# Eighteen weight pieces of a fused attention and FFN kernel: lower ternary side on GpSimd, joined on VectorE

## The reference

```
x = x + cross_attention(layernorm(x), ctx)      # two inner layernorms, one head of width 512, softmax over 256
x = x + ffn(layernorm(x))

def _bitlinear(x, w_latent):                    # used twice in the ffn
    scale = clip(mean(abs(w_latent), axis=1, keepdims=True), 1e-05, None)
    tern = clip(round(w_latent / scale), -1.0, 1.0)
    return x @ (tern * scale).T
h = _bitlinear(x, w_fc) + gate * (x @ v.T @ fast_b.T @ u.T)
y = _bitlinear(relu(h)**2, w_proj)              # w_fc (2048, 512), w_proj (512, 2048)
```

## Time and profile before

| | us |
|---|---|
| median of 3 runs (lowest, highest) | 805.66 (803.67 to 807.49) |
| the profiled execution, its own time | 805.04 |
| its span, from the first to the last instruction | 803.0 |

### The profile page before, as it was taken

How to read it: one execution, slowest core, us unless ns; L and a number is a source line. 1 busy time by engine, 2 the same in 40 slices (tenths; PEclk the granted TensorE clock), 3 DMA queues, 4 the chain that set the end, 5 groups by cost and what they waited for, 6 DMA issues and landing times.

```text
span 803.0 us, 10829 instructions
## 1 busy us (share of the span) xinstructions
PE 777.0 (97%) x3877; PEld 642.9 (80%) x3877; DVE 543.3 (68%) x1100; ACT 374.9 (47%) x705; POOL 150.0 (19%) x171
## 2 busy tenths in 40 slices
PE   6999988999999999999999999999999999999998
PEld 4678767887888778887888788887888788888886
DVE  5998857667757685577766685577766686476434
ACT  5997545335551644326542554326542554424332
POOL 3241130112202022022201122012301122012001
PEclk9999999999999999999999999999999999999999
DMA  9753141034410551134410452124420441021001
GB/s 314 273 144 102 17 77 56 36 54 69 127 40 1 85 112 53 40 46 69 118 57 1 70 86 94 40 36 74 98 83 0 70 75 55 0 35 45 27 0 53
DMA packets 180554, 56.93 MB, mean 71 GB/s; under 512 B 167666, under 2 KB 168068, under 8 KB 180500
## 3 DMA queue, kind: packets, MB, share of 16 engines
q1 hardware_dynamic: 150368, 51.51, 26.2%
q10 hardware_dynamic: 30132, 4.73, 3.4%
HBM read 27.64 MB, written 8.39 MB: 45 GB/s over the span
## 4 chain that ended last, share of the span: by engine, by line
PE 77%; SPq 6%; DVE 5%; ACT 3%; ACTq 3%; DMA 3%; issue 2%; DVEq 0%
PE G L1183 23%; PE O L1299 22%; PE H L1318 22%; SPq L505 5%; ACTq L788 3%; PE H L1324 3%; DVE rbuf L1074 2%; DMA Wv_s<-in_L_xattn_Wv_dram 2%; ACT rbuf L749 1%; PE H L1167 1%; PE G L1265 1%; PE O L1372 1%; DMA n_blocks<-n_rows 1%; PE H L1183 1%; ACT qbuf L757 1%
## 5 line engine op out<-in xcount | busy, mean ns | idle before, releaser
L1299 PE MATMUL O<-projT,qbuf 128*128 128x512 f32 x992 | 246.9, 391 | 6.7 <-DVE qbuf L1078 6.7
L1299 PEld LDWEIGHTS O<-projT,qbuf 128*128 128x128 f32 x992 | 184.1, 188 | 47.7 <-DVE qbuf L1078 10.6
L757 ACT ACTIVATE qbuf<-rbuf 128x512 fp32r<-128x512 f32 x125 | 79.1, 633 | 148.5 <-DVE rbuf L1074 112.1
L1074 DVE TENSOR_TENSOR rbuf<-rbuf 128x512 f32<-128x512 f32 x128 | 95.5, 746 | 61.9 <-ACT rbuf L749 61.8
L1318 PE MATMUL H<-even_group,fcT 128*128 128x512 f32 x512 | 127.8, 392 | 2.9 <-ACT rbuf L749 2.9
L1318 PE MATMUL H<-odd_group,fcT 128*128 128x512 f32 x512 | 127.3, 391 | 0.0
L749 ACT ACTIVATE rbuf<-H,scf 128x512 f32<-128x512 f32 x128 | 86.9, 679 | 68.2 <-PE H L1324 63.2
L1318 PEld LDWEIGHTS H<-even_group,fcT 128*128 128x128 f32 x512 | 94.9, 188 | 22.4 <-ACT rbuf L749 3.3
L1078 DVE TENSOR_TENSOR qbuf<-rbuf,qbuf 128x512 fp32r<-128x512 f32 x125 | 88.8, 710 | 33.7 <-ACT qbuf L757 30.9
L1318 PEld LDWEIGHTS H<-odd_group,fcT 128*128 128x128 f32 x512 | 95.3, 188 | 19.3
L1183 PE MATMUL G<-Wvo,tT 128*128 128x512 f32 x270 | 65.6, 391 | 0.0
(11 more groups left out here) (196 smaller groups left out, 1066.9 us busy)
## 6 DMA issues: line engine op xcount, KB each, us to landing
xb<-in_x_dram SPq DMA_DIRECT2D x8, 1024.0 KB, 4.8
n_blocks<-n_rows SPq DMA_DIRECT2D x112, 64.0 KB, 2.3
ctxb<-in_ctx_dram SPq DMA_DIRECT2D x8, 768.0 KB, 4.3
n_blocks<-ctxb SPq DMA_DIRECT2D x112, 48.0 KB, 2.1
wring<-in_L_ffn_w_fc_dram SPq DMA_DIRECT2D x16, 256.0 KB, 5.3
wring<-in_L_ffn_w_proj_dram SPq DMA_DIRECT2D x16, 256.0 KB, 3.1
out_dram<-x2a SPq DMA_DIRECT2D x8, 512.0 KB, 3.0
x_blocks<-x_rows SPq DMA_DIRECT2D x56, 64.0 KB, 3.0
```

What stands on the lines that cost most here:

```text
L757: nc.scalar.activation(squares(b, j)[:, HI, :], rbuf[:, j % 2, :], ACT.Copy).then_inc(sqhi_made, 1)
L1074: nc.vector.tensor_tensor(rbuf[:, j % 2, :], rbuf[:, j % 2, :], rbuf[:, j % 2, :], ALU.mult).then_inc(square_made, 1)
L1299: mm = pe.matmul(banks[f"O{t}"][:, :], qbuf[:, j % 2, h, t * P:(t + 1) * P], projT[:, j, :], start=(j == 0 and h == HI), stop=(j == NFF - ...
```

## The change

For the 18 pieces 6, 11, 12, 14, 17, 18, 19 and 21 to 31 the lower side is made by GpSimd, in a new step `below:j`, and VectorE's step becomes `join:j`: it waits for the lower side and makes `above` = (w > half) - below in one instruction, the second one of `tern`. The turns of these pieces are then four products in place of eight. The new POOL steps stand between the old ones, in a written order. `below:j` waits for `scale:gr` and for the turn of piece j-4; `join:j` waits for `below:j` alone.

```
     "dve": (
-        "... sides:6 ... sides:11 sides:12 tern:13 wvo:0 sides:14 tern:15 ..."
+        "... join:6 ... join:11 join:12 tern:13 wvo:0 join:14 tern:15 ..."
...                                      (every sides from 6 on becomes a join, in its place)
     "pool": (
-        "scale:0 tb xs23 scale:1 cs23 scale:2 scale:3 scale:4 scale:5 residual:0 residual:1 scale:6 residual:2 "
-        "residual:3 scale:7 a:0 a:1 B.xs23 a:2 a:3 B.cs23 "
+        "scale:0 tb xs23 scale:1 below:6 cs23 scale:2 below:11 scale:3 below:12 below:14 scale:4 below:17 below:18 "
+        "scale:5 below:19 residual:0 below:21 residual:1 below:22 below:23 scale:6 below:24 below:25 residual:2 "
+        "below:26 residual:3 scale:7 below:27 below:28 below:29 below:30 below:31 a:0 a:1 B.xs23 a:2 a:3 B.cs23 "

-JOINED = [int(word[5:]) for word in PROLOGUE["dve"] if word.startswith("tern:")]
+JOINED = [int(word[5:]) for word in PROLOGUE["dve"] if word.startswith(("tern:", "join:"))]
+POOLED = [int(word[6:]) for word in PROLOGUE["pool"] if word.startswith("below:")]

+                    elif st[0] == "below":
+                        j = st[1]
+                        gr, i = j // 4, j % 4
+                        pool.wait_ge(scales_made, gr + 1)
+                        pool.wait_ge(tern_turned, j - 3)
+                        nc.gpsimd.tensor_scalar(below[:, i, :], wring[:, gr % 2, i, :],
+                                                nhalf[:, gr % 2, slice(i, i + 1) if gr < 4 else slice(0, 1)], None, ALU.is_lt
+                                                ).then_inc(below_made, 1)

-                        dve.wait_ge(scales_made, gr + 1)
-                        if j >= 4:
-                            dve.wait_ge(tern_turned, j - 3)
+                        if kind == "join":
+                            dve.wait_ge(below_made, POOLED.index(j) + 1)
+                        else:
+                            dve.wait_ge(scales_made, gr + 1)
+                            if j >= 4:
+                                dve.wait_ge(tern_turned, j - 3)
                         if kind == "tern":
                             link(nc.vector.tensor_scalar(below[:, j % 4, :], w, nhalf[:, gr % 2, row], None, ALU.is_lt))
+                        if kind != "sides":
                             nc.vector.scalar_tensor_tensor(out=above[:, j % 4, :], in0=w, scalar=half[:, gr % 2, row],
                                                            in1=below[:, j % 4, :], op0=ALU.is_gt, op1=ALU.subtract
                                                            ).then_inc(sides_made, 1)
```

More of the change, by code:

```diff
@@ L366, in mk_xattn_ffn @@
         bq_in, bo_in = sem("bq_in"), sem("bo_in")
-        sides_made = sem("sides_made")
+        sides_made, below_made = sem("sides_made"), sem("lower_sides_made")
         sprow_made = sem("sprow_made")
@@ L572, in _ @@
                     move_n1(b + 2)
-            store(6, 0)
+            store(NG - 2, 0)
             for t in range(3):
@@ L1079, in steps @@
                                                 ALU.subtract).then_inc(sqlo_made, 1)
-                    elif kind in ("sides", "tern"):
+                    elif kind in ("sides", "tern", "join"):
                         gr, i = j // 4, j % 4
```

## The result

The changed kernel takes 823.72 us (823.19 to 825.88, 4 runs) beside 804.67 (803.67 to 807.49, 4 runs): 1.0236 times as long [1.0223, 1.0248], slower by 19.0 us. I had said slower by 6.9, in a range from 808.8 to 816.5. The profiled execution has a span of 821.4 us, 18.4 more than before.

What follows compares the result with a forecast made beforehand. PE was taken to bound the whole kernel, but the changed prologue had PE, DVE and ACT full, with DVE's chain after `t:2`. Terms 0.5 + 1.3 + 4.9 + 0.7 - 0.5 = +6.9 us gave 812.6, range 808.8 to 816.5.

Steps and rivals of the forecast that it cites:

- (c): At `join:27`: its lower side stands behind `scale:7` on POOL, so `pT:1` moves by 4.9 us; the largest term.
- the price of a lower side on POOL: Each 128x512 comparison on POOL takes 0.7 us, between 0.5 from smaller instructions and 1.29 from a two-input one.
- (a): Prologue up to `t:0`: late `join:19` delays PE, joined turns give some back; +0.5 us, bounds -1.5 and +1.2.
- (d): At `join:27`: POOL starts `below:28` first and holds the join out for 0.7 us; bounds 0 and 1.3.
- (e): Last joins, 28 to 31: they save 0.5 us, their lower sides running under `xs` and `w`.
- (b): Around `s:0`: `residual:2` and `residual:3` now stand behind `below:25` and `below:26`; +1.3 us, bounds -0.4 and +2.1.
- The lower side costs what two inputs cost: Rival, 12%: each lower side on POOL takes 1.29 us; +9.6 us in all, 815.3.
- TensorE slows down in the gap: Rival, 20%: PE idles some 5 us inside `w:0` and falls to 1.2 GHz; +1.3 to +2.5 more, about 814.5.
- No lock-out: Rival, 13%: POOL's comparison runs beside DVE's without holding it out; +2.3 to +3 us, 808.0 to 808.7.
- Faster: Rival, 3%: the wait of `join:27` vanishes because `scale:7` is ready; -4.0 us, 801.7.
- Bodies: Parts after the prologue, behind `nx0+`: no changed step, every body as long as before, only starting later.

Runs made afterwards that it cites:

- e7: Kernel before plus seven single instructions at GpSimd's idle start, among them the lower side's comparison with 512 and 256 columns: 804.88 us (one run).
- e2: Changed kernel with every lower side on GpSimd made for 8 of 512 columns, order and waits kept: 813.62 us, 1.0113 of the kernel before.
- e3: Changed kernel with only pieces 6, 11, 12, 14, 17, 18, 19 on GpSimd, 21 to 31 as before: 812.02 us, 1.0089 of the kernel before.
- e1: Changed kernel with `below:27` put ahead of `scale:7` on GpSimd, nothing else moved: 817.43 us, 1.0157 of the kernel before.
- e8: Changed kernel with 110 products of the identity filling PE's wait inside `w:0`: 824.37 us, 1.0238 of the kernel before.
- e6: Kernel before plus 18 comparisons on POOL at the change's places, results unused, DVE's and PE's work unchanged: 811.06 us, 1.0068 of the kernel before.
- e10: Changed kernel with only pieces 17 and 18 getting their lower side from GpSimd: 805.72 us, 1.0003 of the kernel before.
- e11: Changed kernel with residuals put ahead of the lower sides that held them up and `below:27` ahead of `scale:7`: 816.43 us, 1.0139 of the kernel before.

## Why the prediction was wrong

The direction was right, and so was (c), the largest term, in its mechanism and its place. The step that failed is **the price of a lower side on POOL**, "I take 0.7 us", bounded by 0.5 and 1.29. It takes 1.56 to 1.59 us where nothing holds it, outside both ends (the changed kernel; alone in e7). Lower sides of over 1.3 us were one of my signs of being wrong. I bounded it from above by an instruction with more inputs and from below by a cast, as if the operation did not matter. The Trainium skill ("GPSIMD Engine Reference", section 3.1), quoted there with 769 ns for 512 elements, would have given half of what e7 measured.

A second step failed beside it, in (a): a join held by what POOL starts next, and a slow clock behind a wait of PE, were thought of only at later places. With 0.31 us in place of 0.7 my working gives some 5.2 us (an estimate from its own terms). e2 measured 9.0, so nearly 4 of the 12 us that I missed are not in the price. In e2 (c) with (d) is 4.5 (8.87 at `pT:1`, 4.36 at `scale:7`) and (e) a gain of 0.4, both close to that working. But `t:2` is 3.2 us late, where it gives nearly nothing.

**(a) up to `t:0`: +5.4 in place of +0.5.** I let `below:12` fall among comparisons at about 1 us with slack to spare. It waits for a turn of PE until 36.97 and then takes some 1.6 us, so `join:12` waited 1.47 us and took 1.18. DVE was 2.5 us late at `crow` (49.23 before, 51.78 after), of which 0.6 was there ahead of the first lower side. e2 shows that this is the price: there `crow` is at 49.58. `join:19` waits for `below:19` behind `scale:5` as I said, 1.85 us where my working has 1.67. But `scale:5` itself begins 2.0 us later, since `abs:23` on ACT is late (50.86 for 48.83), where I had it 0.2 earlier. The lower side is 0.9 longer. And `residual:0` starts right behind it and holds the join for 1.0 us more (1.74 for 0.75), as in e2. I had reasoned so in (b) and (d) and left it out here. Together `n2T:0` starts at 55.98 in place of 50.62. e3 shows this share alone.

Then comes the clock. PE waited 2.91 us for `n2T:0`, and from `n2T:2` into `t:0` its pace was the slow one (the granted clock is 0.50 in 58 to 60 us): `n2T:2` and `n2T:3` take 0.36 us more than before from start to start, and `t:0` 0.7. The twelve products of the turns 17 to 19 take 1.38 us to the start of `t:0`, nearly as long as the 24 before (1.47). So the 0.66 us that I had these joined turns give back were lost to the clock. Up to `t:2` that is some 1.7 us, for which (a) has no term. e3, with the same wait of 2.91 us on PE, shows it as well (`t:0` lasts 4.18).

**(b) the residuals: +2.3 in place of +1.3.** At `s:0`, set against `t:2`, it is 2.3 where my working has 1.9. Right in kind: lower sides and residuals alternate with the joins. The lower side between them was longer (POOL's rows from 71.72 to 75.35). The 0.6 that I had come back behind `s:0` did not: `join:26` met `residual:3` and took 1.66 us, and `scale:7` is 8.5 us late against 6.2 at `t:2`.

**(c) `join:27` behind `scale:7`: +5.8 in place of +4.9.** `pT:1` is 6.2 us later beside the 8.5 of `scale:7`, and 0.4 of them are (d). The wait is 6.19 us, where my working has 5.4 (from 71.26 to 76.63). The excess is the price: `below:27` takes 1.56 from 84.47, where I had 0.7. e2, with a lower side of 0.31 us, gives 4.93, and e1 takes most of the wait away and 6.3 us of the time with it. (a) and (b) put `scale:7` back by 8.5 us in place of 1.8, so their error comes on top.

**(d) `below:28` ahead of `join:27`: 0.43 in place of 0.7.** The join takes 1.18 where 0.75 is its own.

**(e) the last joins: a loss of 2.1 in place of a gain of 0.5.** I had them covered by `xs` and `w`. But `below:29` waits for turns that PE does behind `w` (92.61), and starts at 93.18. From there POOL sets the pace, three lower sides in 4.64 us, and joins 29 to 31 follow it at 1.53 us each. `w:2` is 14.8 us late and `a:0` 16.9. This is the price again: in e2, with short lower sides, these joins gain 0.4 us. I had given the term no bounds.

**The rivals.** *The lower side costs what two inputs cost* was nearest in cause, and it was still too cheap. *TensorE slows down in the gap* happened: the granted clock was 0.50 in 88 to 90 us. It is about 1 us at `nx0+` by e8, just under the 1.3 to 2.5 that I gave it, and filling the gap did not shorten the whole. It happened at `t:0` too, for which I had no term. The earlier trace rows show a pace and not a clock: the clock column of before is 1.00 at 9 to 12 us. My range left out the sum of slow clock and dear lower side, and both came. *No lock-out* is refuted by e6 for comparisons on DVE and by (d) for joins, though the lock is short. *Faster* is far off: its one mechanism asks that `scale:7` be ready when DVE reaches `join:27`, and DVE stood there from 79.9 us on, where `scale:7` ended at 84.5. And in e10, where one join waits for POOL, for 0.38 us, PE's saved passes (0.4 us) brought nothing that can be told.

**Bodies.** 711.5 us in place of 710.4 behind `nx0+`. I had said unchanged. That is the 1.1 between 17.3 and 18.4, and over the runs this stretch lay between 710.0 and 714.6; what moves it was not settled. The granted clock was 0.85 in 110 to 116 us and 0.86 in 128 to 140, where before had 1.00, but e10 has 711.5 too with a mean clock of 0.998.

**Where the 19 us are.** By e2 some 9 do not hang on the length of the instruction, the rest does. Some 1.7 us at `t:0` and about 1 us in `w` are time at the slow clock behind PE's waits. By e1 6.3 hang on one place in POOL's order, but 11.2 stay when the order is put right (e11). By e6 POOL's wide comparisons cost 5.5 us even if nobody waits for their results. These shares overlap and are not to be added.

## What to carry to other kernels

Price an instruction on POOL by a row of the same operation with the same number of columns, or measure it at POOL's idle start first. Scaling from another operation was wrong by more than a factor of two, and two inputs were no upper bound for one. When half of a step moves to a slower engine, list for each piece when its input is ready and when its user comes. A joint step is as late as the slower half together with whatever stands ahead of it in that engine's order, and it can be held by what that engine starts right behind. Each new wait of PE is a place to look for a slow clock. And the passes saved on the engine that is busy 97% of the whole were worth nothing in a stretch where another one sets the end.

## What the hardware showed that I had not expected

POOL's comparison holds DVE out for only part of its time. A join that starts with it takes 1.17 or 1.18 us in place of 0.75, a comparison 0.82 to 0.91 in place of 0.48: 0.35 to 0.43 of POOL's 1.56 us. A second instruction behind it can be held again: `join:12` takes 1.18 and the comparison of `tern:13`, at 39.72 beside the same lower side of POOL, 0.69 for 0.48, 0.64 us together. Beside POOL's addition of two inputs, 1.26 us, a join takes 1.66 to 1.77, and so does L1078 in the earlier trace rows: 0.9 to 1.0 us. The Trainium skill ("SBUF — State Buffer", "Who interferes with whom") has the lock last for a whole instruction. For the addition the rows can be read so, for the comparison they show about a quarter for one instruction of DVE and two fifths for two in a row.

On POOL the number of inputs does not set the price: a comparison of 128x512 with one input takes 1.59 us, an addition with two 1.29, a cast with one 0.84. With an f32 output the comparison took 1.83, beside instructions of DVE.

A gap in mid-kernel slows TensorE, which I had left open: after 5.97 us of idleness the next products ran at a granted clock of 0.50, that is at 1.2 GHz, and at 92 us it was back at 1.00. After 2.91 us of idleness it fell as well: 0.50 in 58 to 60 us. The Trainium skill ("TensorE: Matmul & The Clock Gate", Part 1) says this of an idle array, and the trace agrees.
